# Attention's sums are no longer turned by TensorE: denominators gathered and inverted by themselves, inverses spread through DRAM, product on GpSimd

## The reference

```
h = layernorm(x)
q, k, v = (h @ w.T split into 16 heads of 16, for w in w_q, w_k, w_v)
scores  = q @ k.T / sqrt(16), masked: causal, but the first 196 positions see each other
attn    = softmax(scores);  ctx = attn @ v          # B, heads, S, 16
x = x + layernorm(ctx @ w_o.T + b_o)
x = x + layernorm(ffn(layernorm(x)))                # 8 experts, 2 of them for each token, and one shared
```

## Time and profile before

| what | us |
|---|---|
| median of three runs | 2268.48 |
| profiled execution's own time | 2254.69 |
| its span | 2253.0 |
| PE busy, share of the span | 2077.8, 92% |
| ACT busy | 1701.5, 76% |
| DVE busy | 1477.8, 66% |
| POOL busy | 647.4, 29% |
| attention, from the first exponential to the last | 204.04 to about 1237.7 |

### The profile page before, as it was taken

One profiled execution on the slowest core, in us unless ns is written; L12 is line 12 of the kernel. 1 busy time (PEld: TensorE's weight loads), 2 busy tenths in 40 slices (PEclk: granted clock), 3 DMA queues, 4 the chain that ended last, 5 costly groups with the idle time before them and its releaser, 6 DMA issues. The chain is left out here.

```text
span 2253.0 us, 38463 instructions
## 1 busy us (share of the span) xinstructions
PE 2077.8 (92%) x14097; PEld 1272.1 (56%) x14097; DVE 1477.8 (66%) x2384; ACT 1701.5 (76%) x2165; POOL 647.4 (29%) x645
## 2 busy tenths in 40 slices
PE   7995999999999999999999696999999999999980
PEld 6773333333333333333333686888888888888870
DVE  5663256455556565555565697777788888888877
ACT  5663999999999999999999475333466666666656
POOL 1111000000000000000000353777145565566546
PEclk9996999999999999999999897999999999999995
DMA  6887655555444455554330684574467776677667
GB/s 219 309 296 188 121 69 77 77 74 68 59 59 59 67 77 77 74 74 58 58 59 8 198 289 160 193 259 161 171 204 207 180 181 171 171 172 198 155 180 285
DMA packets 161574, 324.37 MB, mean 144 GB/s; under 512 B 18000, under 2 KB 91856, under 8 KB 155632
## 3 DMA queue, kind: packets, MB, share of 16 engines
q1 hardware_dynamic: 128820, 268.13, 46.2%
q0 software_dynamic: 30256, 46.03, 11.2%
q10 hardware_dynamic: 2316, 7.80, 1.0%
HBM read 198.75 MB, written 127.47 MB: 145 GB/s over the span
## 5 line engine op out<-in xcount | busy, mean ns | idle before, releaser
L1112 ACT ACTIVATE att_prob<-att_scores 128x1024 f32<-128x1024 f32 (+2 forms) x1122 | 1001.3, 1013 | 54.0 <-PE att_scores L1059 49.2
L1078 PE MATMUL att_out<-att_prob,att_va 128*32 128x512 f32 (+3 forms) x5000 | 577.6, 543 | 18.3 <-DVE att_prob L1144 18.2
L1059 PEld LDWEIGHTS att_scores<-att_qs,att_ks 50*128 50x128 f32 x2560 | 209.2, 185 | 486.2 <-ACT att_prob L1112 397.4
L1059 PE MATMUL att_scores<-att_qs,att_ks 50*128 50x512 f32 (+3 forms) x2560 | 458.7, 428 | 21.1 <-PEq L118 17.2
L1830 POOL DMA_INDIRECT sums<-moe_y,moe_token x142 | 307.7, 2167 | 252.1 <-ACT moe_y L2111 207.9
L1144 DVE SCALAR_TENSOR_TENSOR att_prob<-att_prob,att_tri 128x512 f32<-128x512 f32 x224 | 144.7, 687 | 295.5 <-ACT att_prob L1112 295.5
L1010 POOL DMA_DIRECT2D ctx_scr<-att_cout x64 | 48.7, 760 | 987.1 <-DVE att_cout L1194 948.0
L1078 PEld LDWEIGHTS att_out<-att_prob,att_va 128*32 128x32 f32 x5000 | 109.8, 108 | 193.2 <-ACT att_prob L1112 90.0
L1981 PE MATMUL moe_ps<-moe_xt_hi,w_first_hi 128*128 128x512 f32 (+1 forms) x448 | 175.6, 392 | 3.5 <-ACT moe_h L2084 2.2
L1981 PE MATMUL moe_ps<-moe_xt_lo,w_first_hi 128*128 128x512 f32 (+1 forms) x448 | 172.2, 384 | 0.0
L1981 PE MATMUL moe_ps<-moe_xt_hi,w_first_lo 128*128 128x512 f32 (+1 forms) x448 | 172.0, 384 | 0.0
(11 more groups left out here) (295 smaller groups left out, 3901.7 us busy)
## 6 DMA issues: line engine op xcount, KB each, us to landing
qk_parts<-proj_qk SPq DMA_DIRECT2D x64, 512.0 KB, 4.6
keep_first_weights<-w_experts SPq DMA_DIRECT2D x22, 1412.0 KB, 6.6
moe_wraw<-w_experts SPq DMA_DIRECT2D x21, 1412.0 KB, 6.6
att_qs<-qk_parts SPq DMA_DIRECT2D x180, 128.0 KB
att_ks<-qk_parts SPq DMA_DIRECT2D x180, 128.0 KB
moe_rows<-rows_in SPq DMA_DIRECT2D x23, 544.0 KB, 3.8
proj_xin<-x SPq DMA_DIRECT2D x16, 512.0 KB, 3.8
v_scr<-proj_va SPq DMA_DIRECT2D x16, 512.0 KB, 3.5
```

The costliest lines, as they stand in the source:

```text
L1059: last = nc.tensor.matmul(pss[e % SBUFS][:, h, at:at + CH - q0], ks[s][rows, half, kt * P:(kt + 1) * P], qs[s][rows, half, c * CH + q0:(c ...
L1078: last = nc.tensor.matmul(pso[k % 2][strip, q0:], va[team % 2][:, kt, strip], probs_of(u)[:, h, at:at + CH - q0], start=(kt == 0), stop=(i ...
L1112: nc.scalar.activation(probs_of(u)[:, half * 2:half * 2 + 2, start:], pss[e % SBUFS][:, :, start:], ACT.Exp, scale=HD ** -0.5)\
```

## The change

It changes the way from a chunk's sums to the context in DRAM.

- `copy` (DVE) now writes one of three buffers `osb` (before: two), reading PSUM with a step of four elements so that the tokens lie in runs; the denominator's row is now the 17th of each head and not the first, and stands in 16 rows (the values are laid into a tile full of ones).
- SP moves the denominators with a small DMA (`move_denominators`) from 4 rows of 512 to a tile of 32 partitions x 64.
- DVE inverts these (`invert`), in its list 8 units behind the chunk's last unit (`INVERT = COPY + 6`).
- POOL writes the inverses to DRAM, waits, reads them back spread over 128 partitions, waits, multiplies the 128x512 sums by them, and stores the product, not turned, to `ctx_rows` (256 KB with unused rows).
- PE's `turn` and DVE's `finish` go. PE now waits for the copy (`o_copied`) and not for the product before it writes the other PSUM tile again.
- `attention_out` loads the context with features on partitions (`load_features`, two DMAs) and has no transposes in front of the high and low parts. The last chunk (k = 63) is inverted, multiplied and stored inside `attention_out`, at its steps 3 to 7.
- `load_out_first` moves up in SP's list; `zeros` shrinks from 12 rows to 6 for each partition; `frac` and `poly` are allocated later.

The core of the diff (the helper class `Context` only holds the buffers and semaphores):

```diff
+def load_features(eng, to, rows, done):
+    teams = TEAMS // KT
+    for k in range(KT):
+        each = rows[k * teams:(k + 1) * teams].rearrange("a (h r) t -> (a h) r t", r=VA_W)
+        eng.dma_start(to[:, k], each[:, 0:HD]).then_inc(done, 16)
...
-TURN = VALUES + 1
-FINISH = VALUES + 1
+INVERT = COPY + 6
+OBUFS = 3
...
+                for k in range(LAST_K):
+                    n, s = divmod(k, 2)
+                    pool.wait_ge(o.inverted[s], n + 1)
+                    pool.dma_start(o.inv_rows[s], shares[s][:]).then_inc(o.kept[s], 16)
+                    pool.wait_ge(o.kept[s], (n + 1) * 16)
+                    pool.dma_start(inverse[s][:], o.inv_wide[s]).then_inc(o.spread[s], 16)
+                    pool.wait_ge(o.spread[s], (n + 1) * 16)
+                    sums_at = osb[k % OBUFS]
+                    nc.gpsimd.tensor_tensor(sums_at[:], sums_at[:], inverse[s][:], ALU.mult).then_inc(o.c_done, 1)
+                    pool.wait_ge(o.c_done, k + 1)
+                    pool.dma_start(o.place(ctx_rows, k), sums_at[:]).then_inc(o.stored[k % OBUFS], 16)
...
+                def move_denominators(k):
+                    n, s = divmod(k, 2)
+                    sp.wait_ge(o.o_copied, k + 1)
+                    if n:
+                        sp.wait_ge(o.inverted[s], n)
+                    sp.dma_start(dens[s][:], osb[k % OBUFS][HD::VA_W].rearrange("h (r t) -> h r t", r=DEN_ROWS))\
+                        .then_inc(o.moved[s], 16)
+
                 for team in range(1, ALL_TEAMS):
+                    k = (team - 1) * BCH
                     if team > 1:
+                        move_denominators(k - 1)
                         sp.wait_ge(used, (team - 1) * NU)
-                    load_heads(sp, team, slice(0, BCH), loaded[team % 2])
+                    load_parts(sp, team, slice(0, BCH), loaded[team % 2], 0)
+                    move_denominators(k)
+                    load_parts(sp, team, slice(0, BCH), loaded[team % 2], 1)
+                    load_values(sp, team, slice(0, BCH), loaded[team % 2])
                     load_guard(sp, team)
                     if team == 1:
                         sp.wait_ge(z_made, 5)
...
+                    for c in range(1, BCH - 1):
+                        move_denominators(k + c)
...
-                        wait_from_one(pe, c_done, k - 1)
+                        wait_from_one(pe, o.o_copied, k - 1)
...
-                    if r >= TURN and RING_UNITS[r - TURN] in end_of:
-                        turn(end_of[RING_UNITS[r - TURN]])
...
-                    wait_from_one(dve, o_turned, k - 1)
-                    V.tensor_copy(osb[k % 2][:], pso[k % 2][:]).then_inc(o_copied, 1)
+                    wait_from_one(dve, o.stored[k % OBUFS], k // OBUFS * 16)
+                    V.tensor_copy(osb[k % OBUFS][:].rearrange("p (j q) -> p j q", j=TPC),
+                                  pso[k % 2][:].rearrange("p (q j) -> p j q", j=TPC)).then_inc(o.o_copied, 1)
...
+                def invert(k):
+                    n, s = divmod(k, 2)
+                    dve.wait_ge(o.moved[s], (n + 1) * 16)
+                    if n:
+                        dve.wait_ge(o.kept[s], n * 16)
+                    V.reciprocal(shares[s][:], dens[s][:]).then_inc(o.inverted[s], 1)
...
-                for r in range(len(RING_UNITS) + FINISH):
-                    if r >= FINISH and RING_UNITS[r - FINISH] in end_of:
-                        finish(end_of[RING_UNITS[r - FINISH]])
+                for r in range(len(RING_UNITS) + INVERT):
+                    if r >= INVERT and end_of.get(RING_UNITS[r - INVERT], LAST_K) < LAST_K:
+                        invert(end_of[RING_UNITS[r - INVERT]])
```

More of the change, by code:

```diff
@@ L1081, in values @@
                     last.then_inc(used, 1)
-                def turn(k):
-                    pe.wait_ge(o_copied, k + 1)
-                    for j in range(TPC):
-                        last = nc.tensor.transpose(pso[k % 2][:, j * P:(j + 1) * P],
-                                                   osb[k % 2][:, j * P:(j + 1) * P], ident[:])
-                    last.then_inc(o_turned, 1)
-                for r in range(len(RING_UNITS) + TURN):
+                for r in range(len(RING_UNITS) + VALUES):
                     if r < len(RING_UNITS):
@@ L1513, in _ @@
                         projection(k - PROJECT)
-                    if chunk(k):
-                        turn(k)
                     if chunk(k - TURN_BACK):
```

151 lines of the change are left out of this document (87 added, 64 removed).

## The result

The changed kernel takes 2373.80 us (median of five runs, 2364.15 to 2378.03), the kernel before 2268.48 us: a ratio of 1.0464, 95% interval 1.0443 to 1.0484. The forecast was 2289 us, with a range of 2272 to 2309. The direction is right, the size is five times too small and the time is outside the range.

A forecast was written before the change was run, and what follows sets the result against it. ACT was taken to set attention's pace, PE a little ahead. Terms -9 - 6.5 + 19.6 + 16 + 1 = +21 us took the median from 2268.5 to 2289.5, given as 2289 us; range 2272 to 2309.

The forecast's parts named there:

- Turning, -9: Attention: without PE's transposes, two ACT pauses totalling 0.57 us go in 15 teams, gaining 9 us; bounds 0 and 24.
- Border, -6.5: Attention's end to output phase: the next phase starts sooner behind the last copy, gaining 6.5 us; bounds 0 and 9.
- First team, +19.6: Chunk 1's move stands behind four zero stores: 15.6 us delay plus 4 us half-clock restart; bounds 0 and 23.
- Teams 1 to 14, +1.15 us each: Chunk 1's move behind the loads makes its reciprocal and PE's masked block late, +16 us in all; bounds 0 and 35.
- Other waits, nothing: Attention: moves of chunks 0 and 3, POOL's hops and SP's waits cost nothing; POOL's upper bound 1 us a team.
- Output phase, +1: Lost transposes give nothing; low part's two SBUF operands slow GpSimd's roots, plus the last chunk's product: +1 us, bounds 0 to 8.
- That small transfers slip through: Rival: moves pass between the loads without queuing, both stalls vanish, 2254 us; chance 0.19.
- That only the first team stalls: Rival: later teams' moves land by 31 us, so the sum is +5, 2274 us; chance 0.14.
- the rival: POOL's product holds chunk 2's masks in each of 14 teams for 1.3 us, adding 18 us, 2307 us; chance 0.13.
- A margin of 1 us: Teams 1 to 14: chunk 1's move estimated at 32.2 us behind the first load; landing by 31 us means no stall.
- The bound of 2.5 us a team: Teams 1 to 14: upper bound, landing 1.3 us later through a slower copy or POOL's larger transfers, 35 us in all.

The follow-up runs named there:

- e13: Changed kernel with moves between loads, four sum buffers, zero stores spread over teams, idle output-phase transposes, and the next team's values copied seven units later: 2266.76 us, 0.9998.
- e2: Changed kernel with the first team's four zero stores issued behind the moves of chunks 1 and 2: 2362.85 us, 1.0408.
- e5: Changed kernel with chunk 1's move issued ahead of the team's value and guard loads: 2292.08 us, 1.0105.
- e3: Changed kernel without both DMA hops of the inverses and GpSimd's product in attention, sums stored undivided: 2333.28 us, 1.0289.
- e1: Changed kernel with chunk 1's reciprocal four rounds later in DVE's list, behind the masks of chunk 2: 2299.41 us, 1.0128.
- e6: e1 with four buffers of sums instead of three and one buffer of inverses: 2285.81 us, 1.0087.
- e9: Changed kernel with TensorE's eight transposes a chunk put back in the output phase as idle work: 2368.85 us, 1.0417.
- e4: Changed kernel with the output phase's context first copied into PSUM by ACT, high and low parts made from there: 2374.68 us, 1.0473.
- e7: Changed kernel with chunk 1's move issued by ACT on its own queue, two rounds behind the copy: 2302.90 us, 1.0167.
- e10: Changed kernel with chunk 0's move ahead of all loads, chunk 1's before the key loads, four sum buffers, one zero store a team in teams 1 to 4: 2333.16 us, 1.0280.
- e14: Changed kernel with e5's move, zero stores one a team, reciprocals of chunks 0 and 1 four rounds later, four sum buffers, e9's transposes: 2317.89 us, 1.0239.
- e16: e13 with e1's later reciprocal of chunk 1: 2262.59 us (12 runs), 0.9973 to the kernel before.
- e8: Changed kernel with eight more already fulfilled waits in TensorE's list for each of the output phase's 16 projections: 2389.11 us, 1.0537.

## Why the prediction was wrong

The step that failed is the term for the teams 1 to 14. The terms one by one, against the second profile of the kernel before:

- *Turning, -9.* Right: 0.5 us in each undisturbed team of e13, and 0.6 in the changed kernel's last team, where no loads run.
- *Border, -6.5.* Right: -5.8.
- *First team, +19.6.* Right in sum (pauses of 19.2, the team 18.8 longer), partly by luck. PE stood 16.9 us and not 15.6, and the restart cost ACT 2.4 us and not 4: the two errors nearly cancel. The cause was half wrong too: without the zero stores (e2) ACT's pause is still 13.5 us, and with the move ahead of values and guard (e5) 9.8 us, so the loads for team 1 alone are too late for this move. I had put all of it on the stores.
- *Teams 1 to 14, +1.15 us each.* This term failed. The mechanism is the one described, the size is 6.2 us of ACT's pauses (the teams are 5.6 us longer, with the turning's gain of 0.5 taken off). In the mean of the 14 teams the reciprocal starts 35.45 us behind chunk 3's copy, not 32.2: 3.25 us. From there to the masked block it takes 0.3 us more than I took (the reciprocal alone is 0.54 and not 0.3 us), and PE wants the block 0.3 us later than I took, so these two cancel. PE stands 4.3 us instead of 1.15. Then it restarts at half clock: ACT's first pause is in most teams 1.3 us longer than PE's stand, and in six a second pause of 1.07 us follows. That is 1.9 us in the mean of all teams, which I had charged in the first team and forgotten in the later ones. 1.15 + 3.25 + 1.9 = 6.3 us, against 6.2 measured. Fourteen times the missing 5 us are about 70 of the 85 us by which the forecast was off. (My reading of the worst team before was short too: its next window still shows a DMA share of 0.12, so its loads end at 31.2 us and not 30.8. That is too little to matter.)
- *Where the 3.25 us come from.* 1.7 us are POOL's hops, which keep the DMA engines busy longer (e3, and 1.9 us by the DMA shares). The other 1.5 us stay in e3, where the loads end as they did before: from their end to the reciprocal it takes about 2.3 us there (33.7 - 1.3 - 30.1, an estimate), and I had put 0.5 us of tail and 0.5 of landing.
- *Other waits, nothing.* They cost the changed kernel nothing that ACT shows, but they were not nothing. Chunk 0's reciprocal waited up to 3.1 us in the later teams and 10.78 us in the first. In two teams of e1, one of e5 and six of e6 this same wait was 9.5 to 12 us and did cost. Four copies waited for stores (15.7 us in all), which was the next limit in e1.
- *Output phase, +1.* Wrong: +8.5, and by another mechanism. I wrote that DVE runs it without a pause, so that PE's lost transposes give nothing. The trace before shows otherwise: DVE was busy 130 of 156 us in that phase. The lost transposes take something away: without them PE stands longer between projections and runs at half clock longer (e9). The contention, which I priced, is there and costs little (e4).
- *The rivals.* That small transfers slip through fell twice: in SP's queue they wait (e5), and on another queue still for 10 us (e7). That only the first team stalls fell as well: ACT paused in all 14 later ones, for 1.75 to 7.2 us. POOL's products and DVE's work do hold each other. The product takes 2058 ns in the mean where 1.27 us are free, and five of 224 masks (up to 1.77 us instead of 0.69) and 18 steps of the late units (up to 2.31 instead of 1.22) are stretched, 15 us in all; with hops and product left out (e3) none is. But none of the five masks is one of those behind chunk 1's reciprocal, where the rival put them, and e3 bounds hops and product together at 40 us, most of it through the later landing. No run takes the product away alone.

A margin of 1 us stood between "nothing" and a stall, and I priced the stall by the margin. The bound of 2.5 us a team was as narrow, because all its parts came from a trace in which nobody waited: neither a restart at half clock nor the new traffic is in it.

## What to carry to other kernels

A wait put into an in-order list has a deadline, the first instruction behind it that the path needs: price a miss with the restart of the engine that stands (1.9 us here for a stand of 4 us), and where a wait or a transfer is moved, look up the next deadline, since e1, e10, e14 and e16 each ran into one. Work taken off TensorE can slow it where that work filled an idle stretch. Profile the kernel before twice, before looking for 10 us in a phase that the change does not touch.

## What was not expected of the hardware

- A move of 8 KB on a queue of its own starts 9.9 to 11.2 us after issue while another queue keeps the DMA engines full, and 1.2 us after it when they are free (e7).
- TensorE's mean granted clock in the output phase falls from 0.83 (second profile before) to 0.73 when the eight transposes a step go, comes back to 0.82 with idle ones (e9), and falls to 0.68 with eight more waits a step (e8). Seven of PE's stands there are long (3.2 to 6.4 us, in the changed kernel's first 40 and last 25 us of the phase). But the clock falls in the middle too, where no stand is over 1.8 us: in steps 5 to 16 it is 0.94 before with stands of 0.7 us ahead of the projections, 0.84 in the changed kernel with 1.3, and 0.73 in e8 with 1.7.
- GpSimd's 128x512 product takes 1.27 us free and up to 7.33 us beside DVE's work (e6). DVE's masks are stretched in turn, up to 1.8 us instead of 0.69: 18 of them in e5, 15 us in all. In one place of e13 it reached ACT, as a pause of 1.23 us.
